# Summing the heads of a long convolution: one head by GpSimd alone, the other by one strided reduction on VectorE

## The chip, the cores and the metric

The kernel runs on one core of a Trainium2 chip. The core has TensorE (PE, matrix products into PSUM), VectorE (DVE), ScalarE (ACT), GpSimd (POOL) and a queue for transfers (SP, SyncE). They run side by side and wait for one another by semaphores. The metric is the time of one execution on the device in microseconds (us), as the median of several runs.

## The reference, cut to what matters

Two layers are applied to x (8 sequences, 256 channels, 512 positions); each has an attention-like part and a feed-forward part. The change lies in the first part of the first layer, a gated long convolution. With k and v both the context and q the normalised x, in 32 heads of 8 channels:

```python
kv = jnp.einsum('bhil,bhjl->bijhl', k_, v_)
kv_f = jnp.fft.rfft(kv, n=fft_size)
kernel_f = jnp.fft.rfft(ssm_kernel, n=fft_size)
y = jnp.fft.irfft(kv_f * kernel_f, n=fft_size)[..., :L]
out = y + kv * D[None, None, None, :, None]
out = jnp.einsum('bijhl,bhil->bjhl', out, q_)
...
x = x + jnp.tanh(g_xattn[0]) * _L0_xattn_ref(ctx_2048, ctx_2048, _layernorm(x, axis=-1), ...)
```

Since k equals v, the 64 pairs (i, j) of a head are only 36 different ones. Behind it follow a ternary feed-forward part, an attention over the context, and a second feed-forward part.

## The kernel before, in words

The convolution runs over 16 tiles n, each of two heads (hh = 0, 1) of all 8 sequences. Every engine has its own list of instructions, written out by hand in loops over n; no scheduler moves anything.

- **TensorE**, `conv(n)`: 72 small products of head 0 into PSUM banks 0 to 3 (`conv_head(n, 0)`), then 4 transposes that turn the result of tile n-2 (`turn_result`), then 72 products of head 1 into banks 4 to 7. Head 0 waits for the pairs of tile n (`s_kv`), the turned taps (`s_tp`) and the products of tile n-1 on DVE (`s_prod`). In head 1, after 42 products, PE waits for `s_re`: ACT must have copied out the turned result that stood in bank 4.
- **VectorE**, `products(n, hh)`: multiplies the convolved pairs by q in four instructions, so that each of 32 rows (4 blocks of positions by 8 sequences) holds 40 slots (`SLOTS`), five groups of 8 channels. `fold_heads(n, hh)` adds 16 slots to 16 others, in place. Between the two heads DVE takes the statistics of the layernorm of tile n+3 (`ln_sums`).
- **GpSimd**, for each n: `pairs(n+1)` (four instructions that multiply the context by itself), `finish_heads(n-1, 1)` (two additions that leave 8 sums a row in `res`), root and offset of the layernorm of tile n+3, `add_result(n-2)` (the residual), `finish_heads(n, 0)`.
- **ScalarE**: joins the two 16-bit planes of the turned q (`join_q`), squares, normalises x (`norm_q`), splits it into planes (`split_q`), copies out results (`copy_result`), and has in addition the weights of the first feed-forward part: `sum_weight` (sum of absolute values) and `ternary`.
- **SP queue**, in order: x of tile n+4, context of n+2, weights, the transposing transfer of the q planes of tile n+2 (`turn_q_planes`, which waits for `split_q` on ACT), the turned taps of n+2 (`load_toeplitz`, which waits until `conv(n)` is done).

`SLOTS` is 40, `E` 8, `LB` 4, `B` 8, `G` 2. `TOT_STEP` names the tiles 3, 6 and 11, in which PE and DVE also form the mean of a weight.

Of the kernel before, what the change touches and what calls it, by code (L numbers as in the profile page):

```python
# [28 lines left out]
def flamingo_two_layers(nc, xc, cx, ctxt_in, ctx_in, mask, g_xattn, g_ffn, taps_in, dskip, a_w, b_w, out):  # L29
# [10 lines left out]
    G = 2  # L40
# [25 lines left out]
    with ExitStack() as ctx:  # L66
# [144 lines left out]
        s_sq = sem("squares_ready")  # L211
        s_res = sem("heads_reduced")
        s_rt = sem("result_transposed")
# [132 lines left out]
        with nc.Block() as block:  # L346
            @block.sync
            def _(sp):
# [101 lines left out]
                for n in range(NT):  # L450
                    if n + 4 < NT:
                        load_x(n + 4)
                    if n + 2 < NT:
                        load_context(n + 2)
                    for w, first in ((0, 0), (1, 2)):
                        if n in (first, first + 1):
                            load_weight(w, 2 * (n - first))
                            load_weight(w, 2 * (n - first) + 1)
                    if 5 <= n < 9:
                        load_weight(2, n - 5)  # L460
                    if n == 0:
                        sp.wait_ge(s_dadd, 1)
                        sp.dma_start(kpad[:, :], kp_sb).then_inc(s_kpad, 16)
                    if n + 2 < NT:
                        turn_q_planes(n + 2)
                        load_toeplitz(n + 2)
                    if n in B_EARLY:
                        load_b(B_EARLY[n])
                    if n == 15:
                        sp.wait_ge(s_qc, NT)  # L470
                        sp.dma_start(mask_u8, mask.rearrange("b c -> (b c)").rearrange("(a n) -> a n", a=1)
                                     .to_broadcast([P, B * C])).then_inc(s_gate, 16)
                    if n >= NT - 2:
                        turn_x(n + 2 - NT)
# [86 lines left out]
            def _(pool):  # L561
# [31 lines left out]

                def finish_heads(n, hh):
                    pool.wait_ge(s_fold2, 2 * n + hh + 1)
                    if n >= 3:
                        pool.wait_ge(s_rt, n - 2)
                    pr = prod[n % 2][hh]
                    dst = at(res[n % 3].rearrange("p l c -> p (l c)"), hh * E, [[2 * E, LB * B], [1, E]])
                    nc.gpsimd.tensor_tensor(dst, at(pr, 0, [[SLOTS, LB * B], [1, E]]), at(pr, E, [[SLOTS, LB * B], [1, E]]),  # L600
                                            ALU.add).then_inc(s_fold3, 1)
                    pool.wait_ge(s_fold3, 2 * n + hh + 1)
                    nc.gpsimd.tensor_tensor(dst, dst, at(pr, 32, [[SLOTS, LB * B], [1, E]]), ALU.add).then_inc(s_res, 1)  # L603

# [51 lines left out]
                for n in range(NT):  # L656
                    if 1 <= n < NT - 1:
                        pairs(n + 1)
                    if n >= NT - 2:
                        a_integers_x(n + 2 - NT)  # L660
                    if n >= 1:
                        finish_heads(n - 1, 1)
                    if n >= NT - 3:
                        a_norm(n + 3 - NT)
                    if n + 3 < NT:
                        ln_root(pool, 0, n + 3)
                        conv_offset(n + 3)
                    if n >= 2:
                        add_result(n - 2)
                    finish_heads(n, 0)  # L670

                for t in range(NT + 1):
# [6 lines left out]
                    if t == 0:  # L679
                        finish_heads(NT - 1, 1)  # L680
                    if t < NT - 2:
# [36 lines left out]
            def _(pe):  # L718
# [8 lines left out]
                def turn_result(n, to, freed):  # L727
                    pe.wait_ge(s_res, 2 * n + 2)
                    pe.wait_ge(s_prod, freed)
# [594 lines left out]
            def _(dve):  # L1324
                def products(n, hh):
                    dve.wait_ge(s_y, 2 * n + hh + 1)
                    dve.wait_ge(s_qc, n + 1)
                    if n >= 2:
                        dve.wait_ge(s_res, 2 * n - 3 + hh)
                    y = psum[:, 4 * hh:4 * hh + 4, :].rearrange("p l c -> p (l c)")  # L1330
# [13 lines left out]

                def fold_heads(n, hh):
                    dve.wait_ge(s_prod, 2 * n + hh + 1)
                    pr = prod[n % 2][hh]
                    rows = LB * B
                    nc.vector.tensor_tensor(at(pr, 0, [[SLOTS, rows], [1, 16]]), at(pr, 0, [[SLOTS, rows], [1, 16]]),
                                            at(pr, 16, [[SLOTS, rows], [1, 16]]), ALU.add).then_inc(s_fold2, 1)  # L1350

# [20 lines left out]
                def a_product(t, c):  # L1372
# [3 lines left out]
                    if t == 0 and c == 0:  # L1376
                        dve.wait_ge(s_res, 2 * NT - 2)
                    if t == 1 and c == 0:
                        dve.wait_ge(s_res, 2 * NT)
                    if t >= 2 and c == 0:  # L1380
# [182 lines left out]
                for n in range(NT):  # L1563
                    if n in TOT_STEP:
                        a_weight_mean(TOT_STEP[n])
                    products(n, 0)
                    fold_heads(n, 0)
                    if n in TOT_STEP:
# [18 lines left out]
                    if n < NT - 1:  # L1587
                        fold_heads(n, 1)

                for t in range(NT):  # L1590
# [6 lines left out]
                    if t == 0:  # L1597
                        fold_heads(NT - 1, 1)
                        a_scale_x(2)
# [160 lines left out]
```

## Time and profile before

| what | us |
|---|---|
| median of 3 runs | 693.62 (692.9 to 693.78) |
| the profiled execution's own time | 695.11 |
| span of its trace | 693.3 |
| PE busy | 678.9 (98%) |
| DVE busy | 582.7 (84%) |
| ACT busy | 414.9 (60%) |
| POOL busy | 295.0 (43%) |

The convolution takes the first 173 us of the span; the rest is the feed-forward parts and the attention. In the 40 slices of the page (17.3 us each) POOL and DVE are nearly full in the first ten, and POOL is nearly idle at the end, so that its 43% says nothing of the convolution:

```
PE   9989999999999999999999999999999999999997
DVE  5979999999998998998658958889988888898891
ACT  3689999856679989748667444434434434434440
POOL 6869999999765544537400521111110111110000
DMA  8797775553379789998042243363332334342234
```

### The profile page before, as it was taken

Reading aid. Unit: us, or ns where it says so; the run is one execution under the profiler, and the core shown is the slowest. Engines: PE = TensorE matmul, PEld = TensorE weight load, DVE = VectorE, ACT = ScalarE, POOL = GpSimd, SP = SyncE. Lnnn points to the kernel's source line nnn. Section 1 sums busy time; section 2 is a strip of 40 time slices with the busy share of each in tenths; the row PEclk is TensorE's granted clock in tenths of the full one; section 3 lists DMA queues with packets and bytes.
Section 4 is the critical chain, followed back from the end, with each engine's and each line's share of the span. In section 5 each row is a group of like instructions: output and inputs, shape, how many; then the busy total and the mean of one; then the engine's idle time right before and its main releaser. Section 6 shows DMA issues by size and latency. Waiting matters only on the chain.

```text
span 693.3 us, 12921 instructions
## 1 busy us (share of the span) xinstructions
PE 678.9 (98%) x4826; PEld 357.8 (52%) x4826; DVE 582.7 (84%) x1054; ACT 414.9 (60%) x646; POOL 295.0 (43%) x455
## 2 busy tenths in 40 slices
PE   9989999999999999999999999999999999999997
PEld 6756555555444444567754444444444444444445
DVE  5979999998998998658958889988888888898891
ACT  3689999856679989748667444434434434434440
POOL 6869999999765544537400521111110111110000
PEclk9999999999999999999999999999999999999999
DMA  8797775553379789998042243363332334342234
GB/s 296 222 293 209 227 188 141 148 148 111 102 167 194 187 167 201 218 357 308 17 136 17 61 94 75 91 92 92 76 90 41 68 92 92 77 78 59 61 71 112
DMA packets 155390, 94.85 MB, mean 137 GB/s; under 512 B 133825, under 2 KB 134337, under 8 KB 155329
## 3 DMA queue, kind: packets, MB, share of 16 engines
q1 hardware_dynamic: 153600, 90.02, 51.8%
q0 software_dynamic: 1200, 3.93, 1.7%
q8 instruction: 38, 0.62, 0.4%
q14 instruction: 24, 0.19, 0.1%
q10 hardware_dynamic: 528, 0.09, 0.1%
HBM read 53.04 MB, written 8.47 MB: 89 GB/s over the span
## 4 chain that ended last, share of the span: by engine, by line
PE 68%; POOL 15%; DVE 6%; issue 3%; ACT 2%; DMA 1%; SPq 0%; POOLq 0%; ACTq 0%
PE psum L955 29%; PE psum L987 15%; PE psum L882 9%; POOL phase_space L583 5%; PE psum L894 4%; PE psum L938 4%; PE psum L916 4%; POOL phase_space L600 3%; POOL x_sb L607 2%; POOL phase_space L586 2%; POOL phase_space L603 1%; PE psum L740 1%; PE psum L971 1%; DMA x_sb<-x_between 1%; POOL ln_rs L302 1%
## 5 line engine op out<-in xcount | busy, mean ns | idle before, releaser
L955 PE MATMUL psum<-phase_space 128*128 128x512 f16 x1024 | 223.8, 379 | 0.1
L955 PEld LDWEIGHTS psum<-phase_space 128*128 128x128 f16 x1024 | 100.0, 98 | 122.2 <-issue 1.7
L740 PE MATMUL psum<-phase_space 64*64 64x288 f32 x2304 | 150.3, 409 | 6.3 <-POOL phase_space L586 3.5
L740 PEld LDWEIGHTS psum<-phase_space 64*64 64x64 f32 x2304 | 89.9, 134 | 61.0 <-POOL phase_space L586 8.5
L712 POOL DMA_DIRECT2D out<-x_sb x15 | 9.3, 621 | 234.6 <-DVE x_sb L1516 234.6
L987 PE MATMUL psum<-phase_space 128*128 128x512 f16 x480 | 105.7, 379 | 0.0
L1281 ACT ACTIVATE phase_space<-psum,b_scalars 128x512 f32<-128x512 f32 x64 | 43.4, 682 | 75.2 <-PE psum L955 75.1
L1287 ACT ACTIVATE phase_space<-phase_space,magic 128x1024 f32<-128x1024 f32 x32 | 36.4, 1148 | 77.3 <-DVE phase_space L1500 77.3
L882 PE MATMUL psum<-phase_space 128*128 128x512 bf16 (+1 forms) x384 | 78.8, 361 | 0.7 <-DVE phase_space L1343 0.7
L987 PEld LDWEIGHTS psum<-phase_space 128*128 128x128 f16 x480 | 47.0, 98 | 56.6
L1485 DVE SCALAR_TENSOR_TENSOR phase_space<-psum,b_scalars,phase_space 128x512 f32<-128x512 f32 x64 | 47.7, 748 | 28.4 <-ACT phase_space L1281 28.3
L882 PEld LDWEIGHTS psum<-phase_space 128*128 128x128 bf16 x384 | 37.4, 98 | 40.9 <-issue 0.8
L583 POOL TENSOR_TENSOR phase_space<-phase_space 128x512 f32<-128x512 f32 x45 | 48.2, 1097 | 0.0
L1440 DVE TENSOR_REDUCE phase_space<-phase_space 128x8 f32<-128x512 f32 (+1 forms) x32 | 47.4, 1480 | 0.6
L287 DVE BATCH_NORM_STATS2 ln_bn<-x_sb 128x6 f32<-128x512 f32 x64 | 43.5, 680 | 3.0 <-DMA x_sb<-x_between 2.6
L1334 DVE TENSOR_TENSOR phase_space<-psum,phase_space 128x1024 f32<-128x1024 f32 x32 | 39.0, 1220 | 5.6 <-PE psum L740 4.9
L307 POOL TENSOR_SCALAR phase_space<-x_sb,ln_nm,ln_rs 128x512 f32<-128x512 f32 x48 | 38.0, 791 | 12.4 <-POOL ln_rs L302 5.8
L894 PE MATMUL psum<-phase_space 128*128 128x512 bf16 x176 | 40.6, 379 | 1.0 <-issue 0.6
L1147 ACT ACTIVATE phase_space<-psum,a_scalars 128x512 f32<-128x512 f32 (+1 forms) x48 | 30.8, 642 | 14.4 <-PE psum L882 13.1
L314 POOL TENSOR_TENSOR phase_space<-phase_space 128x512 f16<-128x512 f32 x12 | 13.8, 1179 | 59.4 <-ACT phase_space L1293 59.4
L1507 DVE SCALAR_TENSOR_TENSOR phase_space<-phase_space 128x1024 f32<-128x1024 f32 x32 | 37.8, 1223 | 1.3
L1382 DVE SCALAR_TENSOR_TENSOR phase_space<-psum,a_scalars,phase_space 128x512 f32<-128x512 f32 (+1 forms) x48 | 33.2, 696 | 5.9 <-ACT phase_space L1147 4.9
(123 smaller groups left out, 1081.7 us busy)
## 6 DMA issues: line engine op xcount, KB each, us to landing
phase_space<-in_L_weights SPq DMA_DIRECT2D x24, 512.0 KB, 6.0
phase_space<-in_L_weights SPq DMA_DIRECT2D x12, 704.0 KB, 7.1
phase_space<-kpad SPq DMA_DIRECT2D x14, 512.0 KB, 4.3
phase_space<-in_context_heads SPq DMA_DIRECT2D x15, 384.0 KB, 5.2
x_sb<-in_x_tiles SPq DMA_DIRECT2D x16, 256.0 KB, 4.8
phase_space<-in_context_turned SPq DMA_DIRECT2D x8, 512.0 KB, 5.9
x_between<-x_sb SPq DMA_DIRECT2D x16, 256.0 KB
x_sb<-x_between SPq DMA_DIRECT2D x16, 256.0 KB, 6.8
```

The lines of the kernel that those rows point to most:

```text
L287: nc.vector.bn_stats(ln_bn[:, stage, n % 2, :], x_sb[:, n, :]).then_inc(s_ln[stage], 1)
L307: nc.gpsimd.tensor_scalar(dst, x_sb[:, n, :], ln_nm[:, stage, n:n + 1], ln_rs[:, stage, n:n + 1], ALU.add, ALU.mult).then_inc(s_done, 1)
L583: nc.gpsimd.tensor_tensor(at(kv_k, d * E, [[NP, rows], [1, E]]), at(cx_sb[k], 0, [[EX, rows], [1, E]]), at(cx_sb[k], d, [[EX, rows], [1, E ...
L740: return nc.tensor.matmul(at(dst, 0, [[64, B], [1, NP]]), toep[n % 2][row:row + Q, hh, shift:shift + Q], kv[n % 2][row:row + Q, IN_SLOT[j] ...
L882: last = nc.tensor.matmul(bank(UPA[c][part])[:, 0:w], fa_qT[t % 4][:, kk, :], a_wT[part][:, kk, c0:c0 + w], start=(kk == 0), stop=(kk == L ...
L894: last = nc.tensor.matmul(bank(6 + t % 2), fa_hT[t % 2][:, c, :], a_wT[2][:, c, :], start=(c == 0), stop=(c == JA - 1))
L955: last = nc.tensor.matmul(bank(2 * (m % 3) + w), fb_qT[n % 2][:, kk % 2, kk // 2, :], b_wT[w][:, kk // 2, c * 512:(c + 1) * 512], start=(k ...
L987: last = nc.tensor.matmul(bank(6 + k), fb_hT[k][:, part, c, :], b_wT[2][:, c, :], start=(c == 0 and part == 0), stop=(c == JB - 1 and part ...
L1281: nc.scalar.activation(fb_s[m % 2], bank(2 * (m % 3)), ACT.Silu, scale=fb_sm[:, n % 4, 2:3]).then_inc(g_si, 1)
L1334: nc.vector.tensor_tensor(at(pr, 0, [[SLOTS, rows], [E, 4], [1, E]]), at(y, 0, [[64, rows], [1, 32]]), at(q, 0, [[EX, rows], [1, 4], [1, E ...
L1440: nc.vector.tensor_reduce(gx[:, 0, :], grouped(src), AX.X, ALU.max, apply_absolute_value=True).then_inc(s_steps, 1)
L1485: nc.vector.scalar_tensor_tensor(fb_h[n % 2][:, c * 512:(c + 1) * 512], bank(2 * (m % 3) + 1), fb_sm[:, n % 4, 3:4], fb_s[m % 2], ALU.mult ...
```

## The change

Three things change. First, head 1 of a tile is no longer folded on DVE and finished on GpSimd: one `tensor_reduce` on DVE reads all 40 slots of a row in the order "five slots that lie 8 apart, then the next channel" and writes the 8 sums straight to `res`. Second, head 0 is no longer folded on DVE: GpSimd does the fold and both additions itself (`reduce_first_head`), one tile later than its `finish_heads(n, 0)` stood. Third, on the SP queue `turn_q_planes(n + 2)` stands ahead of the weight loads of its step and not behind them. The semaphore `s_res` becomes one for each head.

```diff
@@ SP queue @@
                     if n + 2 < NT:
                         load_context(n + 2)
+                    if 1 <= n < NT - 2:
+                        turn_q_planes(n + 2)
                     for w, first in ((0, 0), (1, 2)):
                         if n in (first, first + 1):
                             load_weight(w, 2 * (n - first))
@@
                         sp.dma_start(kpad[:, :], kp_sb).then_inc(s_kpad, 16)
+                        turn_q_planes(2)
                     if n + 2 < NT:
-                        turn_q_planes(n + 2)
                         load_toeplitz(n + 2)
@@ GpSimd @@
-                def finish_heads(n, hh):
-                    pool.wait_ge(s_fold2, 2 * n + hh + 1)
+                def reduce_first_head(n):
+                    pool.wait_ge(s_prod, 2 * n + 1)
+                    pr = prod[n % 2][0]
+                    rows = LB * B
+                    nc.gpsimd.tensor_tensor(at(pr, 0, [[SLOTS, rows], [1, 16]]), at(pr, 0, [[SLOTS, rows], [1, 16]]),
+                                            at(pr, 16, [[SLOTS, rows], [1, 16]]), ALU.add).then_inc(s_fold2, 1)
...
                     if n >= 1:
-                        finish_heads(n - 1, 1)
+                        reduce_first_head(n - 1)
...
                         add_result(n - 2)
-                    finish_heads(n, 0)
@@ PE @@
-                    pe.wait_ge(s_res, 2 * n + 2)
+                    pe.wait_ge(s_res[0], n + 1)
+                    pe.wait_ge(s_res[1], n + 1)
@@ VectorE @@
-                def fold_heads(n, hh):
...
+                def reduce_second_head(n):
+                    dve.wait_ge(s_prod, 2 * n + 2)
+                    if n >= 3:
+                        dve.wait_ge(s_rt, n - 2)
+                    nc.vector.tensor_reduce(at(res[n % 3].rearrange("p l c -> p (l c)"), E, [[2 * E, LB * B], [1, E]]),
+                                            at(prod[n % 2][1], 0, [[SLOTS, LB * B], [1, E], [E, 5]]), AX.X, ALU.add
+                                            ).then_inc(s_res[1], 1)
...
                     products(n, 0)
-                    fold_heads(n, 0)
...
                     if n < NT - 1:
-                        fold_heads(n, 1)
+                        reduce_second_head(n)
```

GpSimd in one middle tile before: the two `finish_heads` calls are the pairs L600, L603 (head 0, then the pairs of the next tile, then head 1).

```order
L600 TENSOR_TENSOR phase_space<-phase_space 128x32x8
L603 TENSOR_TENSOR phase_space<-phase_space 128x32x8
L583 TENSOR_TENSOR phase_space<-phase_space 128x64x8 x3
L586 TENSOR_TENSOR phase_space<-phase_space 128x64x4
L600 TENSOR_TENSOR phase_space<-phase_space 128x32x8
L603 TENSOR_TENSOR phase_space<-phase_space 128x32x8
L296 TENSOR_SCALAR ln_ve<-ln_ag 128x1
L302 TENSOR_TENSOR ln_rs<-ln_ve,neg_half 128x1
L591 TENSOR_SCALAR ln_off<-ln_ag,ln_rs 128x1
L607 TENSOR_TENSOR x_sb<-x_sb,phase_space 128x512
```

GpSimd in the same tile now (L585 and L588 are the pairs, L600 is the fold, L606 and L609 the two additions, L613 the residual):

```order
L585 TENSOR_TENSOR phase_space<-phase_space 128x64x8 x3
L588 TENSOR_TENSOR phase_space<-phase_space 128x64x4
L600 TENSOR_TENSOR phase_space<-phase_space 128x32x16
L606 TENSOR_TENSOR phase_space<-phase_space 128x32x8
L609 TENSOR_TENSOR phase_space<-phase_space 128x32x8
L296 TENSOR_SCALAR ln_ve<-ln_ag 128x1
L302 TENSOR_TENSOR ln_rs<-ln_ve,neg_half 128x1
L593 TENSOR_SCALAR ln_off<-ln_ag,ln_rs 128x1
L613 TENSOR_TENSOR x_sb<-x_sb,phase_space 128x512
```

Two additions of 32x8 have gone from each tile, and one of 32x16 has come.

VectorE over one middle tile before, from head 1 to the statistics behind the next head 0 (L1349 is `fold_heads`):

```order
L1334 TENSOR_TENSOR phase_space<-psum,phase_space 128x32x32
L1336 TENSOR_TENSOR psum<-psum,phase_space 128x32x24
L1338 TENSOR_TENSOR phase_space<-psum,phase_space 128x32x8
L1343 TENSOR_TENSOR phase_space<-phase_space,psum 128x32x3x8
L1349 TENSOR_TENSOR phase_space<-phase_space 128x32x16
L1334 TENSOR_TENSOR phase_space<-psum,phase_space 128x32x32
L1336 TENSOR_TENSOR psum<-psum,phase_space 128x32x24
L1338 TENSOR_TENSOR phase_space<-psum,phase_space 128x32x8
L1343 TENSOR_TENSOR phase_space<-phase_space,psum 128x32x3x8
L1349 TENSOR_TENSOR phase_space<-phase_space 128x32x16
L287 BN_STATS ln_bn<-x_sb 128x6
L289 BN_AGGR ln_ag<-ln_bn 128x2
```

VectorE over the same stretch now (L1340 to L1349 are the four instructions of `products`, L1355 is the reduction):

```order
L1340 TENSOR_TENSOR phase_space<-psum,phase_space 128x32x32
L1342 TENSOR_TENSOR psum<-psum,phase_space 128x32x24
L1344 TENSOR_TENSOR phase_space<-psum,phase_space 128x32x8
L1349 TENSOR_TENSOR phase_space<-phase_space,psum 128x32x3x8
L1355 TENSOR_REDUCE phase_space<-phase_space 128x32x8
L1340 TENSOR_TENSOR phase_space<-psum,phase_space 128x32x32
L1342 TENSOR_TENSOR psum<-psum,phase_space 128x32x24
L1344 TENSOR_TENSOR phase_space<-psum,phase_space 128x32x8
L1349 TENSOR_TENSOR phase_space<-phase_space,psum 128x32x3x8
L287 BN_STATS ln_bn<-x_sb 128x6
L289 BN_AGGR ln_ag<-ln_bn 128x2
```

Both folds are gone, and one reduction stands behind head 1; it writes 256 sums a partition out of 1280 values.

The SP queue in step n = 1 (L355 context, L378 the q planes, L384 weights, L366 taps):

```order
 L355 DMA phase_space<-in_context_heads 128x768
+L378 DMA_TRANSPOSE phase_space<-phase_space 128x8x128
 L384 DMA phase_space<-in_L_weights 128x1408 x2
-L378 DMA_TRANSPOSE phase_space<-phase_space 128x8x128
 L366 DMA phase_space<-kpad 128x2x512
```

The transposing transfer has moved ahead of two weight loads, which now wait behind it.

## Rows read from the trace of the kernel before

**Rows 1.** Page, part 4: the chain that ended last, by engine.

```profile
PE 68%; POOL 15%; DVE 6%; issue 3%; ACT 2%; DMA 1%; SPq 0%; POOLq 0%; ACTq 0%
```

**Rows 2.** Timeline of PE: start us, us, engine, line, operation, xcount [idle before <-releaser].

```profile
32.26 0.63 PE L732 MATMUL psum<-ident,phase_space 128*128 128x128 f32 x4 [0.26 <-DVE phase_space L1343]
38.20 7.99 PE L740 MATMUL psum<-phase_space 64*64 64x288 f32 x102 [2.26 <-ACT phase_space L1114]
46.36 0.63 PE L732 MATMUL psum<-ident,phase_space 128*128 128x128 f32 x4
...
55.82 0.66 PE L732 MATMUL psum<-ident,phase_space 128*128 128x128 f32 x4
...
65.30 0.66 PE L732 MATMUL psum<-ident,phase_space 128*128 128x128 f32 x4
...
75.03 0.38 PE L866 MATMUL psum<-tot,ones 128*128 128x1 f32 x2
...
160.84 6.69 PE L740 MATMUL psum<-phase_space 64*64 64x288 f32 x102 [0.52 <-ACT phase_space L1114]
167.46 0.66 PE L732 MATMUL psum<-ident,phase_space 128*128 128x128 f32 x4
...
176.96 1.47 PE L882 MATMUL psum<-phase_space 128*128 128x384 bf16 x8 [0.34 <-DVE phase_space L1343]
```

**Rows 3.** Timeline of POOL in a middle tile.

```profile
96.82 3.11 POOL L583 TENSOR_TENSOR phase_space<-phase_space 128x512 f32<-128x512 f32 x3
...
99.89 1.17 POOL L586 TENSOR_TENSOR phase_space<-phase_space 128x256 f32<-128x256 f32 x1
...
101.02 0.74 POOL L600 TENSOR_TENSOR phase_space<-phase_space 128x256 f32<-128x256 f32 x1
...
105.05 1.20 POOL L600 TENSOR_TENSOR phase_space<-phase_space 128x256 f32<-128x256 f32 x1
...
107.02 3.12 POOL L583 TENSOR_TENSOR phase_space<-phase_space 128x512 f32<-128x512 f32 x3
```

**Rows 4.** Timeline of PE in that tile.

```profile
101.12 4.59 PE L740 MATMUL psum<-phase_space 64*64 64x288 f32 x72 [0.49 <-POOL phase_space L586]
```

**Rows 5.** Timeline of DVE in that tile.

```profile
95.58 1.23 DVE L1334 TENSOR_TENSOR phase_space<-psum,phase_space 128x1024 f32<-128x1024 f32 x1
...
99.02 1.46 DVE L1349 TENSOR_TENSOR phase_space<-phase_space 128x512 f32<-128x512 f32 x1
...
100.40 0.68 DVE L287 BATCH_NORM_STATS2 ln_bn<-x_sb 128x6 f32<-128x512 f32 x1
...
104.67 0.97 DVE L1349 TENSOR_TENSOR phase_space<-phase_space 128x512 f32<-128x512 f32 x1
...
105.78 1.23 DVE L1334 TENSOR_TENSOR phase_space<-psum,phase_space 128x1024 f32<-128x1024 f32 x1
```

**Rows 6.** Groups by line and form: xcount, busy us, mean ns of one, idle before.

```profile
L1440 DVE TENSOR_REDUCE phase_space<-phase_space 128x32 f32<-128x2048 f32 x16 | 36.6, 2286 | 0.6
L1388 DVE TENSOR_REDUCE a_scalars<-phase_space 128x1 f32<-128x1408 f32 x16 | 25.9, 1618 | 0.5
```

**Rows 7.** Timeline of SP and ACT in step n = 1.

```profile
23.61 0.90 SPq L384 DMA_DIRECT2D phase_space<-in_L_weights  x2
...
29.10 1.24 SPq L378 DMA_TRANSPOSE phase_space<-phase_space  x1
...
32.85 2.08 ACT L1081 ACTIVATE phase_space<-phase_space 128x512 uint16<-128x512 uint16 x4 [1.10 <-issue]
```

**Rows 8.** Line L378, the transposing transfers of the q planes.

```profile
DMA to landing us min/median/max: 2.8/3.6/5.5
```

**Rows 9.** Stretch: us, then PE, PEld, DVE, ACT, POOL busy (x), PEclk, DMA share, GB/s.

```profile
39.00:40.00 1.00, 1.00 (x12) 0.50 (x8) 0.00 (x0) 1.00 (x3) 0.98 (x2) 0.50 1.38 342
```

**Rows 10.** Timeline of DVE in tile 13, behind its products.

```profile
155.63 0.69 DVE L1364 TENSOR_REDUCE a_scalars<-phase_space 128x1 f32<-128x512 f32 x1 [0.52 <-POOL phase_space L307]
...
157.43 0.66 DVE L1349 TENSOR_TENSOR phase_space<-phase_space 128x512 f32<-128x512 f32 x1
```

More of the change, by code:

```diff
@@ L211, in flamingo_two_layers @@
         s_sq = sem("squares_ready")
-        s_res = sem("heads_reduced")
+        s_res = [sem(f"heads_reduced{hh}") for hh in range(G)]
         s_rt = sem("result_transposed")
@@ L592, in conv_offset @@
                                             ALU.mult, ALU.mult).then_inc(s_off, 1)
-                def finish_heads(n, hh):
-                    pool.wait_ge(s_fold2, 2 * n + hh + 1)
+                def reduce_first_head(n):
[4 more added lines that the diff above has]
+                                            at(pr, 16, [[SLOTS, rows], [1, 16]]), ALU.add).then_inc(s_fold2, 1)
                     if n >= 3:
                         pool.wait_ge(s_rt, n - 2)
-                    pr = prod[n % 2][hh]
-                    dst = at(res[n % 3].rearrange("p l c -> p (l c)"), hh * E, [[2 * E, LB * B], [1, E]])
-                    nc.gpsimd.tensor_tensor(dst, at(pr, 0, [[SLOTS, LB * B], [1, E]]), at(pr, E, [[SLOTS, LB * B], [1, E]]),
+                    dst = at(res[n % 3].rearrange("p l c -> p (l c)"), 0, [[2 * E, rows], [1, E]])
+                    pool.wait_ge(s_fold2, n + 1)
+                    nc.gpsimd.tensor_tensor(dst, at(pr, 0, [[SLOTS, rows], [1, E]]), at(pr, E, [[SLOTS, rows], [1, E]]),
                                             ALU.add).then_inc(s_fold3, 1)
-                    pool.wait_ge(s_fold3, 2 * n + hh + 1)
-                    nc.gpsimd.tensor_tensor(dst, dst, at(pr, 32, [[SLOTS, LB * B], [1, E]]), ALU.add).then_inc(s_res, 1)
+                    pool.wait_ge(s_fold3, n + 1)
+                    nc.gpsimd.tensor_tensor(dst, dst, at(pr, 32, [[SLOTS, rows], [1, E]]), ALU.add).then_inc(s_res[0], 1)
                 def add_result(n):
@@ L679, in _ @@
                     if t == 0:
-                        finish_heads(NT - 1, 1)
+                        reduce_first_head(NT - 1)
                     if t < NT - 2:
@@ L1328, in products @@
                     if n >= 2:
-                        dve.wait_ge(s_res, 2 * n - 3 + hh)
+                        dve.wait_ge(s_res[hh], n - 1)
                     y = psum[:, 4 * hh:4 * hh + 4, :].rearrange("p l c -> p (l c)")
@@ L1343, in products @@
                     nc.vector.tensor_tensor(side, side, at(y, NP, [[64, rows], [E, 3], [1, E]]), ALU.add).then_inc(s_prod, 1)
-                def fold_heads(n, hh):
[L1346 to L1350, printed above, removed]
+                def reduce_second_head(n):
[5 more added lines that the diff above has]
+                                            ).then_inc(s_res[1], 1)
                 def a_weight_mean(w):
@@ L1376, in a_product @@
                     if t == 0 and c == 0:
-                        dve.wait_ge(s_res, 2 * NT - 2)
+                        dve.wait_ge(s_res[0], NT - 1)
                     if t == 1 and c == 0:
-                        dve.wait_ge(s_res, 2 * NT)
+                        dve.wait_ge(s_res[0], NT)
                     if t >= 2 and c == 0:
@@ L1597, in _ @@
                     if t == 0:
-                        fold_heads(NT - 1, 1)
+                        reduce_second_head(NT - 1)
                         a_scale_x(2)
```

## The prediction

> **What bounds the kernel now.** I read the chain of waits first. PE holds 68% of it and POOL 15% [rows 1]. PE's share cannot be touched by this change, so POOL's is the question, and it lies wholly in the convolution. The timeline of PE comes next, by its transposes (L732), which stand once in each tile. Between 55.82 and 65.30 a tile takes 9.48 us: PE runs through and that is its own work [rows 2]. From 65.30 to 167.46, ten tiles, it is 102.16 us or 10.2 a tile [rows 2], 7.36 us more than ten times 9.48. Then POOL's timeline for the middle tile: its rows follow one another from 96.82 to 107.02, a period of 10.20 us with no idle time named [rows 3], and PE's head 0 waited 0.49 us for the last of the pairs, L586 [rows 4]. So POOL sets the pace of the middle. The period is longer than 9.48 by more than that wait, since each wait also empties PE's pipeline.
>
> DVE is full too: from 95.58 to 105.78 it has the same 10.20 us, but 1.38 of them are the first fold and what it waits for (99.02 to 100.40), and 1.11 the second and the start of the next tile (104.67 to 105.78) [rows 5]. These two L1349 have the same size and last 1.46 and 0.97 us. The longer one starts under POOL's third L583 and ends at 100.48; POOL's L586 starts at 99.89 and takes 1.17 us for 256 elements, where L600 takes 0.74 for as many [rows 3, 5]. The two engines block one another there. What DVE does without the folds is 10.20 - 1.38 - 1.11 = 7.71 us.
>
> The early part has its own stall. In tile 2 PE waits 2.26 us for ACT's copy of the first result, and the tile up to the next transposes takes 46.36 - 32.26 = 14.10 us [rows 2]. Behind the stall the granted clock is 0.50, the lower level of 1.2 GHz [rows 9], and the 102 products take 7.99 us, against 6.69 for 102 behind a wait of 0.52 in tile 14 [rows 2]: 1.3 us for the clock.
>
> **POOL's side.** Removed in a tile: one pair L600 and L603, from 105.05 to 107.02, 1.97 us [rows 3]. Also gone is what L586 lost to the fold on DVE, 1.17 - 0.74 = 0.43. Added: a fold of 128x512; L583 has that size and takes 3.11/3 = 1.04 us [rows 3], with a wait for it 1.12. POOL's load becomes 10.20 - 1.97 - 0.43 + 1.12 = 8.92 us, under PE's 9.48. What would then be late next on POOL is its wait for the layernorm of tile n+3, about 4.4 us behind the end of PE's head 0; the pairs of n+2 are done some 7 us after that, and PE needs them two tiles after the head began, so 3 to 4 us of slack remain. In this stretch POOL gets out of PE's way.
>
> **DVE's side: the disputed cost.** The reduction reads 1280 values a partition. No row shows one with a step of 8 values between neighbours. The nearest are contiguous: 1618 ns for 1408 values and 2286 for 2048 in 32 groups [rows 6], so (2286 - 1618)/640 = 1.044 ns a value, and 1618 - 128 x 1.044 = 1484 ns for 1280. That is the lower end: nothing about a step can make it faster than contiguous reading. The upper end is 2.96 us, four additions of 256 elements at GpSimd's 0.74 [rows 3], the slowest such work in the trace. I take 1.48, the value of the nearest rows. DVE's load is then 7.71 + 1.48 = 9.19 us, 0.29 under PE's 9.48. It becomes the bound at 9.48 - 7.71 = 1.77 us.
>
> A possible block by GpSimd would come on top. The Trainium skill, page "SBUF — State Buffer", section "Who interferes with whom", says that a DVE instruction with two SBUF inputs contends with a GpSimd instruction that reads SBUF, and that `tensor_reduce` never does on this chip. By that rule, the trace agrees on the first half (1.46 against 0.97 us [rows 5]); without it the new reduction would lose up to 0.5 a tile and DVE would stand at 9.7.
>
> **The middle's gain.** Of the 7.36 us, 2 x 0.38 are products for a weight's mean in tiles 6 and 11 (L866, x2 [rows 2]) and stay: 6.6 remain. The last tiles keep some. In tiles 12 to 14 DVE has 1.80 us more behind its products (155.63 to 157.43, the first feed-forward tile's scale and statistics [rows 10]). Behind head 1 it then has 3.44 + 1.80 + 1.48 = 6.7 us (3.44 for a head's products, 95.58 to 99.02 [rows 5]) in a gap of about 4.45, is 2.3 late for the next head 0, and PE, which can bear 1.5, waits some tenths in tiles 13 and 15. And ACT's copy, for which PE waited 0.52 at 160.84 [rows 2], hangs on that same scale and on DVE, not on POOL; it comes hardly earlier while PE does, so I leave 1.1 us there. Together 1.5 stay: the middle gains 5.1. In the first feed-forward tile DVE has the last reduction, 1.48 instead of a fold, in front of products for which PE waits: minus 0.5.
>
> **The order of the transfers.** In step 1 the transposing transfer is issued at 29.10 in either order, since it waits for ACT's `split_q`; two weight loads of 704 KB, issued at 23.61, are then still in flight [rows 7]. ACT waited 1.10 us for it before 32.85 [rows 7], so it landed 3.7 us after issue; the fastest of 14 took 2.8 [rows 8]. With nothing in front it lands at 31.9 and ACT's wait is 0.2: ACT gains 0.9, and so does the copy that PE waits for. Whether a stall of 1.4 still lowers the clock no row tells (0.52 did not, 2.26 did [rows 2, 9]); I count half of 1.3. This term is 0.9 + 0.65 = 1.55, bounds 0 and 2.4. What the queue now holds back are the weight loads (issued near 30.4, not 23.6) and the taps behind them; ACT wants those weights some 7 us later, which is about what they need. Later steps have several us of slack for both.
>
> **The sum.** 5.1 - 0.5 + 1.55 = 6.15 us, from 695.11 to 689.0 for an execution like the profiled one. That one lies 1.5 above the median of the runs; from the median 693.62 it gives 687.4. Behind the convolution PE runs without such waits for long stretches, and the DMA waits there hang on this kernel's own stores, so the gain is carried to the end.
>
> **Rivals.**
> *The reduction is slow, DVE becomes the bound.* A value that lies 32 bytes from the last costs two steps: 148 + 1280 x 2.09 = 2.82 us. DVE's tile is 7.71 + 2.82 = 10.53 us, and 11.5 in the three tiles with 1.80 more and no layernorm (0.82 less). From the transposes at 46.36, taken 1.55 earlier, ten tiles of 10.53 and three of 11.5 end at 184.7, less about 0.7 for terms counted twice, where before stood 176.96 [rows 2]: 7 us slower, 700.6. It loses from about 2.2 us for the reduction on. For it: no row shows such a step and the margin is only 0.29. Against it: `products` read and write 40-slot rows at about one value a cycle (1.23 us for 1024 [rows 5]), though in runs of 8.
> The Trainium skill, page "Advanced Engine Details and Errata", section "Memory Cachelines", speaks for this rival: SBUF lines have 16 bytes and an engine needs at least two hits on a line to hide the memory's latency. Each of the five slots lies in a line of its own. No run here shows it.
> *In between.* The reduction takes 1.8 to 2.2 us, or GpSimd blocks it: at 2.05 the tiles take 9.76 and 10.74, the end of the convolution is 174.7, a gain of 2.3, 691.3.
> *The transfers cost.* The taps of tile 3 come behind 1408 KB of weights, 4.1 us at the 342 GB/s of [rows 9], and PE waits for them up to 2 us. Then the third term is -0.5 and the time 689.5.
> *It does nothing.* ACT also has near 9.5 us of work in tiles with weights, and PE's pace could come from there: 692.5 to 694.
>
> **How the numbers follow.** Forecast 0.50, between and transfers together 0.18, slow reduction 0.27, nothing 0.05. The measurement can tell about 0.2%, 1.4 us. Faster is the first two less a small part, 0.67; within 0.2% 0.05; slower 0.28. The likeliest case's own range is 684.8 (the clock kept, nothing left in the last tiles) to 689.8. The slow case holds more than 2 in 10, so the range goes up to it: 684.8 to 700.8.
>
> **What would show it.** Right: the reduction near 1.5 us; ten tiles between transposes near 9.5 us; POOL idle before the layernorm of tile n+3; the L586 of before at 0.74 and not 1.17; PE's wait in tile 2 under 1.5 us. Wrong: a reduction over 1.8 us, DVE without idle time and PE waiting for its last product instruction; PE waiting for the taps in tile 3; a wait of PE for ACT in every tile.

## The result, and the profile after

The changed kernel takes 697.36 us (median of 5 runs, 696.56 to 697.84) against 693.62 (5 runs, 692.9 to 693.82): a ratio of 1.0055, with a 95% interval of 1.004 to 1.0069. It is slower by 3.7 us; the forecast was 687.4, faster by 6.2. The range held the time only through the slow case at its end. The profiled execution took 697.58 us, its span is 695.8.

The page first: the engines' busy time, and below it the chain that ended last.

```profile
PE 677.7 (97%) x4814; PEld 360.9 (52%) x4826; DVE 590.9 (85%) x1038; ACT 414.4 (60%) x646; POOL 279.9 (40%) x439
...
PE 67%; DVE 17%; issue 5%; ACT 3%; DMA 3%; POOL 0%; SPq 0%; ACTq 0%
...
L1355 DVE TENSOR_REDUCE phase_space<-phase_space 128x256 f32<-128x1280 f32 x16 | 40.2, 2510 | 0.3
```

POOL has left the chain (15% in [rows 1]) and DVE has come in its place, from 6% to 17%. The last row shows the reduction: it takes 2510 ns on average, where the forecast had 1480.

The timeline of DVE in the same middle tile as [rows 5]:

```profile
94.29 2.53 DVE L1355 TENSOR_REDUCE phase_space<-phase_space 128x256 f32<-128x1280 f32 x1
96.72 1.22 DVE L1340 TENSOR_TENSOR phase_space<-psum,phase_space 128x1024 f32<-128x1024 f32 x1
...
99.18 0.95 DVE L1349 TENSOR_TENSOR phase_space<-phase_space,psum 128x768 f32<-128x768 f32 x1
100.05 0.69 DVE L287 BATCH_NORM_STATS2 ln_bn<-x_sb 128x6 f32<-128x512 f32 x1
...
103.33 0.95 DVE L1349 TENSOR_TENSOR phase_space<-phase_space,psum 128x768 f32<-128x768 f32 x1
104.32 2.50 DVE L1355 TENSOR_REDUCE phase_space<-phase_space 128x256 f32<-128x1280 f32 x1
```

From one reduction to the next it is 10.03 us with no idle time named. POOL in the same tile, which answers to [rows 3]:

```profile
96.48 0.73 POOL L588 TENSOR_TENSOR phase_space<-phase_space 128x256 f32<-128x256 f32 x1
97.16 1.27 POOL L600 TENSOR_TENSOR phase_space<-phase_space 128x512 f32<-128x512 f32 x1
...
101.04 0.19 POOL L296 TENSOR_SCALAR ln_ve<-ln_ag 128x1 f32<-128x1 f32 x1 [0.92 <-DVE ln_ag L289]
```

POOL now waits for DVE, 0.92 us here and 0.9 to 1.0 in each of the middle tiles, and the last of the pairs is back at 0.73 us (1.17 in [rows 3]). PE, from the first transposes (L738) on, answers to [rows 2] and [rows 4]:

```profile
28.38 4.60 PE L746 MATMUL psum<-phase_space 64*64 64x288 f32 x72 [1.04 <-DVE phase_space L1349]
32.90 0.65 PE L738 MATMUL psum<-ident,phase_space 128*128 128x128 f32 x4
37.79 6.53 PE L746 MATMUL psum<-phase_space 64*64 64x288 f32 x102 [1.18 <-ACT phase_space L1120]
44.50 0.64 PE L738 MATMUL psum<-ident,phase_space 128*128 128x128 f32 x4
...
85.11 0.66 PE L738 MATMUL psum<-ident,phase_space 128*128 128x128 f32 x4
...
100.28 4.60 PE L746 MATMUL psum<-phase_space 64*64 64x288 f32 x72 [0.32 <-DVE phase_space L1349]
...
145.02 0.66 PE L738 MATMUL psum<-ident,phase_space 128*128 128x128 f32 x4
151.59 4.60 PE L746 MATMUL psum<-phase_space 64*64 64x288 f32 x72 [1.39 <-DVE phase_space L1349]
...
166.97 0.66 PE L738 MATMUL psum<-ident,phase_space 128*128 128x128 f32 x4
...
173.50 4.70 PE L888 MATMUL psum<-phase_space 128*128 128x512 bf16 x23 [1.35 <-DVE phase_space L1349]
...
185.99 4.70 PE L888 MATMUL psum<-phase_space 128*128 128x512 bf16 x23 [1.77 <-DMA phase_space<-phase_space]
191.31 2.53 PE L900 MATMUL psum<-phase_space 128*128 128x512 bf16 x11 [0.61 <-issue]
```

In the middle PE waits for DVE and no longer for POOL. The places at which it loses most lie elsewhere: at the start (28.38), in tile 13 (151.59) and in the first feed-forward tiles (173.50, 185.99).

To say where 3.7 us went, the profiled execution of before is a bad partner: it took 695.11 us, 1.5 more than the median, and the last experiment shows a dip of PE's clock in it that two others don't have. A second execution of the same kernel (693.2 us, span 691.4) lies near the median. PE in it:

```profile
32.36 0.63 PE L732 MATMUL psum<-ident,phase_space 128*128 128x128 f32 x4 [0.26 <-DVE phase_space L1343]
37.45 6.53 PE L740 MATMUL psum<-phase_space 64*64 64x288 f32 x102 [1.41 <-ACT phase_space L1114]
44.15 0.63 PE L732 MATMUL psum<-ident,phase_space 128*128 128x128 f32 x4
...
83.32 0.66 PE L732 MATMUL psum<-ident,phase_space 128*128 128x128 f32 x4
...
144.43 0.66 PE L732 MATMUL psum<-ident,phase_space 128*128 128x128 f32 x4
...
165.41 0.66 PE L732 MATMUL psum<-ident,phase_space 128*128 128x128 f32 x4
171.16 3.40 PE L882 MATMUL psum<-phase_space 128*128 128x512 bf16 x15 [0.56 <-DVE phase_space L1343]
...
187.43 2.53 PE L894 MATMUL psum<-phase_space 128*128 128x512 bf16 x11 [0.67 <-issue]
```

| up to | before | after | after is behind by | gained or lost here |
|---|---|---|---|---|
| first transposes | 32.36 | 32.90 | 0.54 | 0.54 lost |
| second transposes | 44.15 | 44.50 | 0.35 | 0.19 gained |
| sixth | 83.32 | 85.11 | 1.79 | 1.44 lost |
| twelfth | 144.43 | 145.02 | 0.59 | 1.20 gained |
| fourteenth | 165.41 | 166.97 | 1.56 | 0.97 lost |
| first feed-forward product | 171.16 | 173.50 | 2.34 | 0.78 lost |
| third feed-forward tile (L894, L900) | 187.43 | 191.31 | 3.88 | 1.54 lost |

The spans differ by 4.4, so 0.5 more comes later. What gains are the six tiles in which POOL held before back, and a little the tile with the reordered transfer; everywhere else the changed kernel pays. Each column is one execution: in a third execution of before the sixth transposes stand at 84.19 and the twelfth at 144.94, so a single row of the table can be off by some 0.9 us; the total is surer (4.4 in the spans, 3.7 in the medians).

### The profile page after: what moved, and what is told of

Its sections match the earlier page's. It is cut to its first block, busy times and chain, and to the rows that moved or that the text cites. A ratio compares the mean times of both kernels' runs of the same rounds, so it can differ in the third digit from the quotient of the medians.

```text
span 695.8 us, 12888 instructions
## 1 busy us (share of the span) xinstructions
PE 677.7 (97%) x4814; PEld 360.9 (52%) x4826; DVE 590.9 (85%) x1038; ACT 414.4 (60%) x646; POOL 279.9 (40%) x439
## 4 chain that ended last, share of the span: by engine, by line
PE 67%; DVE 17%; issue 5%; ACT 3%; DMA 3%; POOL 0%; SPq 0%; ACTq 0%
PE psum L961 27%; PE psum L993 14%; PE psum L888 10%; PE psum L900 5%; PE psum L944 4%; DVE phase_space L1340 4%; PE psum L922 4%; DVE psum L1342 3%; DVE phase_space L1349 3%; DMA phase_space<-phase_space 2%; PE psum L746 1%; DVE phase_space L1447 1%; DVE phase_space L1355 1%; DVE phase_space L1344 1%; DVE phase_space L1514 1%
## 5 line engine op out<-in xcount | busy, mean ns | idle before, releaser
L746 PEld LDWEIGHTS psum<-phase_space 64*64 64x64 f32 x2304 | 94.2, 133 | 57.6 <-issue 13.1
L585 POOL TENSOR_TENSOR phase_space<-phase_space 128x512 f32<-128x512 f32 x45 | 46.8, 1066 | 0.0
L900 PE MATMUL psum<-phase_space 128*128 128x512 bf16 x171 | 40.0, 379 | 1.1 <-issue 0.6
L1355 DVE TENSOR_REDUCE phase_space<-phase_space 128x256 f32<-128x1280 f32 x16 | 40.2, 2510 | 0.3
L1340 DVE TENSOR_TENSOR phase_space<-psum,phase_space 128x1024 f32<-128x1024 f32 x32 | 39.0, 1218 | 1.3 <-PE psum L746 1.3
```

What stands on the lines that cost most here:

```text
L585: nc.gpsimd.tensor_tensor(at(kv_k, d * E, [[NP, rows], [1, E]]), at(cx_sb[k], 0, [[EX, rows], [1, E]]), at(cx_sb[k], d, [[EX, rows], [1, E ...
L746: return nc.tensor.matmul(at(dst, 0, [[64, B], [1, NP]]), toep[n % 2][row:row + Q, hh, shift:shift + Q], kv[n % 2][row:row + Q, IN_SLOT[j] ...
L900: last = nc.tensor.matmul(bank(6 + t % 2), fa_hT[t % 2][:, c, :], a_wT[2][:, c, :], start=(c == 0), stop=(c == JA - 1))
L1340: nc.vector.tensor_tensor(at(pr, 0, [[SLOTS, rows], [E, 4], [1, E]]), at(y, 0, [[64, rows], [1, 32]]), at(q, 0, [[EX, rows], [1, 4], [1, E ...
L1355: nc.vector.tensor_reduce(at(res[n % 3].rearrange("p l c -> p (l c)"), E, [[2 * E, LB * B], [1, E]]), at(prod[n % 2][1], 0, [[SLOTS, LB * ...
```

## Experiments

### Which property of the reduction costs

The theory was that the distance between neighbours costs. The reduction of tile n reads its values at a distance of n % 8 + 1 values of 4 bytes.

```diff
-  at(prod[n % 2][1], 0, [[SLOTS, LB * B], [1, E], [E, 5]])
+  at(prod[n % 2][1], 0, [[SLOTS, LB * B], [1, E], [n % 8 + 1, 5]])
```

> The changed kernel, but the reduction of tile n reads its five values n % 8 + 1 apart instead of 8 apart (steps of 4 to 32 bytes, two tiles for each), so the sums of the second head are wrong ones. Step theory: the duration grows with the step, about 1.5 us where neighbours share a 16-byte line (steps 1 and 2) and 2.5 us from step 4 on, where none do. Rival, short groups: 256 outputs of 5 values cost the same 2.5 us at any step. Rival, GpSimd blocks it: the duration scatters with what GpSimd does in that tile and not with the step.

Timeline of DVE, line L1355 of that kernel, tiles 0 to 8:

```profile
22.25 1.49 DVE L1355 TENSOR_REDUCE phase_space<-phase_space 128x256 f32<-128x1280 f32 x1
31.21 1.49 DVE L1355 TENSOR_REDUCE phase_space<-phase_space 128x256 f32<-128x1280 f32 x1
42.09 2.02 DVE L1355 TENSOR_REDUCE phase_space<-phase_space 128x256 f32<-128x1280 f32 x1
52.13 2.57 DVE L1355 TENSOR_REDUCE phase_space<-phase_space 128x256 f32<-128x1280 f32 x1
62.21 2.54 DVE L1355 TENSOR_REDUCE phase_space<-phase_space 128x256 f32<-128x1280 f32 x1
...
92.48 2.52 DVE L1355 TENSOR_REDUCE phase_space<-phase_space 128x256 f32<-128x1280 f32 x1
102.51 1.49 DVE L1355 TENSOR_REDUCE phase_space<-phase_space 128x256 f32<-128x1280 f32 x1
```

A distance of 1 or 2 values costs 1.49 us, 3 cost 2.02, and from 4 values (16 bytes) on it is 2.5 and grows no more. The same numbers come back from tile 8 on. The groups of five are the same in all, so they don't make the difference. Nor does GpSimd: in the changed kernel's trace the reduction at 94.29 runs beside GpSimd's pairs and takes 2.53 us, and the one at 178.33, with GpSimd idle from 177.34 to 182.68, takes 2.44. The Trainium skill, page "Advanced Engine Details and Errata", section "Memory Cachelines", gives SBUF lines of 16 bytes and asks for two hits on a line. On where the cost begins the trace agrees; the size is 2.51/1.49 = 1.7 times, for which the section has no figure.

### The same kernel with a cheap reduction

Neighbours side by side in all tiles; the sums are then not the head's, all else is as changed.

```diff
-  at(prod[n % 2][1], 0, [[SLOTS, LB * B], [1, E], [E, 5]])
+  at(prod[n % 2][1], 0, [[SLOTS, LB * B], [5, E], [1, 5]])
```

> The changed kernel with the reduction reading five neighbouring slots instead of five slots 8 apart, the same 1280 values; the sums of the second head are wrong ones. It is the kernel that the forecast priced. Step theory: the reduction takes 1.5 us, DVE has idle time, the tiles between transposes take near 9.5 us, and the time is 687 to 689. Rival, short groups: 2.5 us and 697.

The reduction took 1482 ns on average, the forecast's own 1.48, and the kernel 689.75 us (689.6 to 689.9), 0.995 of before (0.9935 to 0.9964). So 1.03 us a reduction are worth 697.36 - 689.75 = 7.6 us (7.3 by the two ratios to before, which were taken at different times), and the step of the reduction is the whole difference between faster and slower. It is 3.5 us faster than before and not 6.2, so other terms of the sum were too large as well.

### The order of the transfers, alone and undone

The first kernel is the one before with the new order on SP; the second is the changed one with the old order, that is, with the edit below undone.

```diff
@@ before, new order @@
+                    if 1 <= n < NT - 2:
+                        turn_q_planes(n + 2)
                     for w, first in ((0, 0), (1, 2)):
...
+                        turn_q_planes(2)
                     if n + 2 < NT:
-                        turn_q_planes(n + 2)
                         load_toeplitz(n + 2)
```

> The kernel before with only the q planes' transfer moved ahead of the weight loads. If the 2.5 us that tile 3 gained come from the order, this is 692 to 693, with PE's wait in tile 2 near 1.2 us and no stretch at the lower clock. If they come from the shorter work of GpSimd, it is 693.6 and the wait is 2.3 us.

> The changed kernel with the transfers in the order of before. If the order is what gained in tile 3, this is slower than the changed kernel, 698 to 699. If the order is what lost (weights late), it is faster, 695.

The new order alone: 692.64 us (10 runs), ratio 0.9988 (0.9978 to 0.9997). Undone in the changed kernel: 697.81 (4 runs, 697.65 to 699.28) against 697.36. Alone it is worth 0.6 us. In the changed kernel the difference of 0.45 is not clear of the noise: the ratios to before, 1.007 (1.0055 to 1.0086) and 1.0055 (1.004 to 1.0069), overlap. In the kernel before with the new order PE's wait in tile 2 is 0.76 us:

```profile
36.70 6.53 PE L742 MATMUL psum<-phase_space 64*64 64x288 f32 x102 [0.76 <-ACT phase_space L1116]
43.40 0.64 PE L734 MATMUL psum<-ident,phase_space 128*128 128x128 f32 x4
```

### Additions in place of the reduction

If a step of 32 bytes is the trouble, three additions on VectorE that read channels side by side should be cheap. The code is shortened: `pr[0:16]` stands for slots 0 to 15 of each row, and `dst` for the 8 sums in `res`.

```diff
-  nc.vector.tensor_reduce(... [E, 5] ...)
+  nc.vector.tensor_tensor(pr[0:16], pr[0:16], pr[16:32], ALU.add)
+  nc.vector.tensor_tensor(dst, pr[0:8], pr[8:16], ALU.add)
+  nc.vector.tensor_tensor(dst, dst, pr[32:40], ALU.add)
```

> The second head of the changed kernel is summed by VectorE alone, but with three additions (512, 256 and 256 values out, in runs of 8 or 16 channels that lie side by side) in place of the reduction in steps of 8 values. Theory (the step of 32 bytes is what costs): an undisturbed fold of 128x512 took 0.66 us in the trace of before, so the three take about 0.66 + 0.4 + 0.4 = 1.5 us where the reduction takes 2.5; VectorE's tile falls from 10.0 to 9.0 us, under PE's 9.48, and the time goes to 690 to 691.5, about that of the contiguous reduction (689.75). Rival (additions with two inputs are blocked by GpSimd, which the reduction is not): the three together take 2.3 us or more in the middle tiles, GpSimd's pairs or fold grow too (the last of the pairs from 0.73 back towards 1.17 us), tiles stay at 10 us or more, and the time is 696 to 699. In between (1.9 us): 693.

It took 706.02 us, ratio 1.0195 (1.0176 to 1.0213). That the step costs stands by the first two experiments; what fell is that the additions are cheap, and the rival was still too mild. Timeline of DVE behind head 1 of a middle tile:

```profile
98.60 0.71 DVE L1359 TENSOR_TENSOR phase_space<-phase_space 128x512 f32<-128x512 f32 x1
99.34 1.15 DVE L1362 TENSOR_TENSOR phase_space<-phase_space 128x256 f32<-128x256 f32 x1
100.53 1.22 DVE L1365 TENSOR_TENSOR phase_space<-phase_space 128x256 f32<-128x256 f32 x1
```

and of POOL beside it:

```profile
97.72 3.75 POOL L586 TENSOR_TENSOR phase_space<-phase_space 128x512 f32<-128x512 f32 x3
101.43 0.91 POOL L589 TENSOR_TENSOR phase_space<-phase_space 128x256 f32<-128x256 f32 x1
```

The small additions take 1.15 and 1.22 us beside POOL's pairs, and 0.42 behind the last tile of this same trace, where POOL is idle. The first, larger addition is not held back here (0.71, and 0.68 with POOL idle), but the three pairs that run beside all this take 3.75 instead of 3.12. The sum is 3.08 us, longer than the reduction it replaces, and a tile takes 10.65. The reduction never showed this: in the changed kernel its 16 instances lie between 2435 and 2552 ns whatever POOL did. The Trainium skill, page "SBUF — State Buffer", section "Who interferes with whom", says that a VectorE instruction with two SBUF inputs contends with a GpSimd instruction that reads SBUF, and that a `tensor_reduce` does not on this chip; by that rule, the trace agrees on both halves.

### The wait in the third feed-forward tile

PE waits 1.77 us before this tile's products (185.99 in the profile after). In the order of VectorE's instructions the last reduction stands ahead of the scale of x for that tile; here the scale goes first.

```diff
-                        reduce_second_head(NT - 1)
                         a_scale_x(2)
+                        reduce_second_head(NT - 1)
```

> In the first feed-forward tile the scale of x for tile 2 stands ahead of the last reduction and not behind it; nothing else differs from the changed kernel. Theory (the reduction of 2.4 us stands on the chain VectorE scale - ScalarE quantise - GpSimd - transposing transfer - PE of tile 2, where PE waited 1.77 us): the wait falls below 0.5 us and the time by about 1.4 us, to 696.0 against 697.4 of the changed kernel. Rival (the late chain of that tile comes from the end of the convolution being late anyway, or PE then waits for the last result's transposes): the time stays within 0.4 us of 697.4.

697.42 us (696.79 to 698.21): nothing. The chain that I had named did get shorter, GpSimd had its integers 2.4 us earlier, but PE then waited for another instruction of VectorE, which stands behind the reduction in either order:

```profile
185.78 4.91 PE L888 MATMUL psum<-phase_space 128*128 128x512 bf16 x24 [1.55 <-DVE phase_space L1389]
```

With the three additions as well:

> Both edits together: three additions on VectorE for the second head, and the scale for tile 2 ahead of the last of them. If both theories hold the time is that of the kernel with three additions less up to 1 us (the additions hold the scale back by 1.5 us rather than 2.4): 689.5 to 691. If additions are blocked by GpSimd: 695 to 698. If the late scale makes no difference: as with three additions alone, within 0.4 us.

705.79 us (704.97 to 707.16), as with the additions alone.

### Sharing the work out

Five kernels divide the sums between the two engines in other ways. In `SHARED` tiles of the first three, head 1 is folded by VectorE and finished by GpSimd, as before. The edits are given in words.

```diff
+  SHARED = (0, 1, 2, 12, 13, 14, 15)   # ends; mixed: and 6, 10; GpSimd alone: all
+  if n in SHARED: fold on VectorE, two additions on GpSimd
+  else:           tensor_reduce on VectorE
```

> The changed kernel, with head 1 of tiles 0 to 2 and 12 to 15 alone summed as before. Theory (what the reduction costs at the ends is the whole loss, the middle being faster than before): the tile behind the first transposes loses its wait of 1.04 us for VectorE, the last tiles and the first feed-forward tile theirs, about 3 us together: 694.4 against 697.4; the middle tiles stay at 10.0 us. Rival (the ends are limited by the layernorm's scale and ScalarE, not by the reduction): within 0.8 us of 697.4.

> The changed kernel, with head 1 of tiles 0, 1, 2, 6, 10 and 12 to 15 summed as before (VectorE folds 16 slots, GpSimd makes the two additions), the reduction in the other seven. Theory (VectorE's tile of 10.0 us is the bound in the middle and the reduction is what is late at both ends): as e9_ends, and in tiles 6 and 10 VectorE is 1.8 us shorter while GpSimd is 1.5 to 2.0 longer and uses the 0.9 us of idle time it has in each tile; the average middle tile goes from 10.03 to about 9.7, 2 us more gained than by e9_ends: 692.4, faster than before. Rival (the two engines take the time back by blocking one another, as the three additions did): no better than e9_ends, 694 or more.

> The part on GpSimd alone: head 0 by GpSimd as changed, head 1 of all tiles as before, no reduction. Theory (GpSimd was the bound of before and gets a fold of 1.27 us more in each tile): GpSimd's tile goes to 11.2 us, one us above before, and the time to about 705. Rival (what is lost in the changed kernel comes from the part on GpSimd): about 697.4 or a little more, as the changed kernel.

The ends alone: 696.68 us (6 runs, 695.44 to 698.11), 0.7 less than the changed kernel and not 3, which is within the spread of the two. In the trace GpSimd's share of the sums (2.7 us for head 0, 1.5 for head 1) stands in front of its layernorm at the end of the convolution, for which VectorE then waits:

```profile
166.15 0.69 DVE L1403 TENSOR_REDUCE a_scalars<-phase_space 128x1 f32<-128x512 f32 x1 [1.69 <-POOL phase_space L316]
```

That wait explains a part. PE has its fourteenth transposes at 165.29 us there, 1.7 earlier than in the changed kernel, and its third feed-forward tile at 190.15, still 1.2 earlier; but this execution (697.9 us) loses the 1.2 again behind the convolution, in longer waits for transfers (0.94 and 1.32 us, where the changed kernel's has 0.56 and 0.56). How much of that is in every execution is open.

Mixed: 696.11 (695.53 to 696.81), only 0.6 less again, where its theory had 692.4. GpSimd alone: 706.2 (705.88 to 706.68), ratio 1.0186 (1.0171 to 1.02), as expected: its middle tiles take 11.15 us. So the part on GpSimd by itself costs 13 us, and the reduction, slow as it is, takes 9 of them back and leaves 4.

The last two start from before with the new order and use the reduction in a few middle tiles only; `REDUCED` lists them, and the comment has the list of the second kernel.

```diff
+  REDUCED = (5, 8, 11)                 # half: 4, 6, 8, 10, 12
```

> The kernel before with the transfers in the new order, and the reduction on VectorE in place of fold and two additions for head 1 of tiles 5, 8 and 11 only; all else as before (both heads of the other tiles folded by VectorE, finished by GpSimd). Theory (the two engines are to be balanced: GpSimd's 10.2 us a tile lose 1.97 in every third, and VectorE's gain 2.5 - 1.0 in them): GpSimd's average is 9.54, VectorE's 7.7 + 1.5 + 0.5 = 9.7, so middle tiles average 9.7 to 9.8 against 10.2, over 8 tiles 3.4 us less, and the ends are as before: 689.5 against 692.6 with the new order alone, which would be as good as the contiguous reduction. Rival (VectorE is as full as GpSimd in these tiles, so a tile with a reduction takes what its neighbours save): 692 to 693.

> As e11_third, with the reduction in tiles 4, 6, 8, 10 and 12. Theory: VectorE's average is 7.7 + 1.4 + 0.75 = 9.85 and is the bound, with GpSimd at 9.2: tiles of 9.9, 2.5 us less than the new order alone, so 690.2, a little worse than a third. Rival: as for e11_third, 692 to 694, the slower the more tiles are reduced.

A third: 692.84 (11 runs, 691.41 to 693.94), ratio 0.9989 (0.998 to 0.9999), the same as the new order alone. Half: 696.55 (695.87 to 697.68), slower than even its rival had said (692 to 694). The balance of loads that I had worked out is not reached. Busy times of 60 to 145 us (columns as in [rows 9]), first the new order alone, then a third:

```profile
60.00:145.00 85.00, 81.94 (x1248) 48.56 (x1244) 82.12 (x110) 77.98 (x117) 81.40 (x101) 1.00 0.68 185
```

```profile
60.00:145.00 85.00, 83.35 (x1278) 52.17 (x1274) 83.62 (x110) 79.75 (x120) 75.48 (x97) 1.00 0.68 186
```

POOL falls from 81.40 to 75.48 us, but DVE, which stood at 82.12 of 85, goes to 83.62. Two engines were full, not one, and every way to relieve POOL that I tried fills DVE. Of all versions that compute the reference, the new order alone and that with a third are the fastest, and neither can be told from before by the 0.2% bound.

### The execution that was profiled

> The kernel before, unchanged, profiled again. Theory (the first profiled execution had a longer stall of PE in tile 2 and the lower clock behind it, which most executions don't have, and that is its distance of 1.5 us from the median): a run near 693.3 shows PE waiting for ScalarE in tile 2 by less than 2 us, no stretch at 1.2 GHz behind it, and the third transposes near 45 rather than 46.36 us. Rival (the stall is in every execution, and the distance lies elsewhere): wait and lower clock as in the first profile, with a run of 693.3 or of 695.

> The same once more, since one execution can't tell how often the stall comes: by the theory the run's time and the third transposes go together, 1.3 to 1.5 us apart between executions with and without the lower clock; by the rival the third transposes stand at 46.3 again whatever the time.

The kernel before, twice more: 693.2 and 693.62 us, spans 691.4 and 691.8. PE's wait in tile 2 was 1.41 and 2.03 us, with no lower clock behind either; the second transposes (which the expectation calls the third) stood at 44.15 and 44.74 and not at 46.36 [rows 2]. The stretch that answers to [rows 9] in the first of them:

```profile
39.00:40.00 1.00, 1.00 (x24) 0.64 (x20) 0.33 (x1) 1.00 (x2) 0.90 (x3) 1.00 1.32 149
```

The granted clock is 1.00, 2.4 GHz, where it was 0.50. So one of three profiled executions had the dip of the clock, and the dip (7.99 us for the 102 products, 6.53 in the other two) is most of that one's distance from the others. It is probably no single event: of 49 further runs of before, 41 took 692.51 to 693.9 us and eight took 694.39 to 695.32, seven of these with a mean granted clock of 0.996 to 0.998 (the others have 0.998 to 1.0). None of the eight has a trace, so that the dip is in them is not shown.

## Why the prediction was wrong

**The reduction (the step that failed).** I took r = 1.48 us, "the value of the nearest rows". It is 2.51. The bounds, 1.48 and 2.96, held it. With r = 1.48 the kernel is 3.5 us faster than before, with 2.51 it is 3.7 slower: 7 us for one number of which no row spoke. By a straight line through these two points it breaks even near 2 us, against 2.2 in the forecast. The kernel with eight distances lies on that line: its reductions take 2.20 us on average, for which the line gives 695.1, and its one run took 695.31. The rule that spoke against the lower value was quoted, and got 0.27; the rows for the other side were contiguous readings, which bear on this question least of all.

**The slow rival** had the mechanism: DVE becomes the bound, back to back, POOL idle for a part of each tile, PE waiting for the last product instruction. Its price, 2.82 us and 700.6, was too high: it doubled the cost of each value, and the measured duration is 1.7 times and grows no more beyond 16 bytes.

**DVE's tile.** 7.71 + r was 7.52 + r (10.03 - 2.51). Right within 0.2.

**POOL's side.** The added fold took 1.27 us, 1.42 with the wait for it, and not 1.12. Its price came from a multiplication of as many values (L583, 1.04); the trace of before also had an addition of as many values in place, the residual L607, at 1280 ns, which was the nearer row. The L586 of before went to 0.73 as said, and POOL became idle before the layernorm of tile n+3, as said: its load is 10.03 - 0.92 = 9.11 us, for 8.92. This half was right in the main and earned nothing, since DVE took over.

**The middle's gain, 5.1.** The ten tiles of the sum, from the fourth transposes to the fourteenth, take 160.76 - 63.90 = 96.86 us with the cheap reduction and 164.98 - 62.83 = 102.15 with the new order alone: a gain of 5.3, near the forecast. But the fourteenth transposes come only 4.2 earlier, because 1.1 us are lost ahead of these tiles. There, in the kernel with the cheap reduction, ACT waits for a transfer and PE for ACT's copy:

```profile
52.07 2.11 ACT L1087 ACTIVATE phase_space<-phase_space 128x512 uint16<-128x512 uint16 x4 [2.89 <-DMA phase_space<-phase_space]
...
57.44 6.53 PE L746 MATMUL psum<-phase_space 64*64 64x288 f32 x102 [0.75 <-ACT phase_space L1120]
```

With the new order alone ACT waits 0.87 us at this place and PE not at all. Both are single executions. In the second execution of before the ten tiles take 101.33, and the gain is 4.5.

**The end, -0.5.** The last product of the convolution and the first feed-forward tiles lose about 1.1 with the cheap reduction and 2.3 with the real one (0.78 + 1.54 in the table).

**The order of the transfers, 1.55.** It is 0.6. In the kernel before with the new order the mechanism is as said: ACT starts on the planes 3.2 us after the transfer's issue (28.17 to 31.34) and PE's wait is 0.76 us, where the two later executions of before have 3.9 and 3.7 us and waits of 1.41 and 2.03. In the changed kernel's own profile it is not: 4.2 us from issue to start (28.28 to 32.44), and a wait of 1.18, against 1.48 in the profile with the order undone. Why the transfer is no faster there is open. And the 0.65 for the clock were read from an execution that was not typical, and I took them off the median. With the sizes measured, 4.2 - 1.1 + 0.6 = 3.7, against 3.5 measured for r = 1.48.

## What to carry to other kernels

Where one operation decides the sign and no row shows its access pattern, take the rule that speaks against it as the likelier price, or leave the sign open; rows of the same operation with another pattern are no evidence. When the bound is moved from one engine to another that is nearly as full, the first question is what the second one's busy time is without idle time, over the same stretch, not over the span. And look whether the profiled execution is as long as the median: where it isn't, find the stall that makes the difference before pricing its removal.

## What the runs showed of the hardware

- A VectorE `tensor_reduce` of 1280 f32 values in groups of five: 1.49 us at a distance of 4 or 8 bytes, 2.02 at 12, 2.5 at 16 and beyond, up to 32; about 0.8 ns more a value.
- A VectorE addition of 256 values with both inputs in SBUF took 0.42 us with GpSimd idle and 1.15 to 1.22 beside GpSimd's multiplications: the delay, 0.75 us, is longer than the addition. One of 512 took 0.68 with GpSimd idle and, beside the same multiplications, 1.46 in the kernel before but 0.70 with the three additions, where the multiplications got longer instead (3.75 us for three, otherwise 3.12).
- GpSimd's fold of 512 values in rows of 40 took 1.27 us and its residual addition of 512 values 1.28, where its multiplications of 512 take 1.04 [rows 3]; whether the operation, the writing in place or the pattern makes the difference was not tried.
